# Another order for the opening and step 4 of a fused attention and FFN layer

## The chip, the cores and the metric

The kernel runs on one core of one Trainium2 chip. The metric is the device time of one launch in microseconds, shown as the median of three runs. TensorE (PE) does matrix products, VectorE (DVE) elementwise work and transposes, ScalarE (ACT) activations and copies, GpSimd (POOL) elementwise work, and SyncE (SP) issues all the DMAs of this kernel, one after the other.

## The reference

One post-norm transformer layer on x of shape (8, 1024, 512), all float32:

```python
q, k, v = x @ Wq.T + bq, x @ Wk.T + bk, x @ Wv.T + bv    # 16 heads of 32
q, k = rope(q), rope(k)
qk = einsum('bshd,bstd->bsht', q, k) / sqrt(32)    # heads against heads, at the same position
out = einsum('bsht,bstd->bshd', softmax(qk), v)
out = swapaxes(out, 1, 2).reshape(B, S, E)
x = layernorm(x + out @ Wo.T + bo)
g, u = (x @ gate_w.T) * gate_s, (x @ up_w.T) * up_s    # 512 -> 1408
x = layernorm(x + ((silu(g) * u) @ down_w.T) * down_s)
```

The attention is over the 16 heads of one position, so its matrices are 16 by 16. The projections and the FFN hold most of the arithmetic.

## The kernel before

The 8192 positions are 64 tiles of 128. **Attention** takes two tiles as one unit, 32 units in all. A float32 product is made of three products: each operand is split into a high part (a copy rounded to the matrix type, made by ScalarE) and a low part (operand minus high part), and `project` adds high·high, high·low and low·high over four blocks of the contraction: 12 matmuls of 512 columns for one tile and one weight. A unit needs 96 of them: q, k and v of two tiles (`project_qk`, `project_v`), and the output projection of two tiles (`project_heads`); besides 128 small matmuls of 64 columns for the scores (`score`) and 128 for the weighted values (`weigh_values`).

The work of a unit is spread over five **steps**: step s loads and splits x of unit s, projects and rotates unit s-1, does the softmax and the weighted values of unit s-2, the output projection and the residual of unit s-3, and the norm of unit s-4. Each engine has its own `step` with a fixed order of calls; waits on semaphores (`wait_ge`) tie the engines together, and an engine that waits does nothing that stands behind the wait. `unit_steps` (L78) runs step 4 (`OPENING` is 4) as straight code, then steps 5 to 31 as a hardware loop, then step 32. What steps 0 to 3 would do is written out by hand for each engine: this is the **opening**. In `step` a Python flag `late` changes the order for step 4 alone.

Beside the attention the kernel prepares the **FFN weights**. They arrive in 32 slabs, one in each step. SyncE loads slab m into six operands of `f_all` (`ffn_slabs`); `pieces_of(m)` gives the pieces, 8, 6, 11 and 9 for slabs 0 to 3, and `halved` cuts them further until there are 13 for each slab, so that one semaphore `f_loaded` can be counted in a loop. GpSimd makes four sums (`sums_of_slab`), ScalarE the high parts (`high_of_slab`), GpSimd the low parts (`low_of_slab`, 128x792), ScalarE looks for the largest low part (`top_of_slab`), and SyncE stores high and low parts in four DMAs, which wait for `f_lo_done`, ahead of the loads of the next slab.

Other names that the prediction uses. VectorE: `add_bias` (L1376) takes a projection out of PSUM, `sines` (L1383) is half of the rotation, `turn_k`, `turn_q`, `turn_prob` are transposes, `subtract_top` / `sums_of_prob` / `scale_prob` are the softmax, `low_of_heads` (L1439) makes the low part of the attention's output, `low_of_weight` (L1342) that of a weight (four instructions of 128x512), `add_residual` adds x and takes statistics. ScalarE: `split_x`, `spread_k` (L940), `exponent` (L964), `spread_p` (L980), `high_of_heads`. GpSimd: `rotate` (L1195 and L1201), `low_x` (L1173), `add_output_bias` (L1189), `rstd_of`. `spread_p` makes the operand that `weigh_values` waits for, `spread_k` that of `score`. The number in brackets is the unit, then the tile in it, then the weight (1 is k, 0 is q).

After the attention come eight super steps of the **FFN**, in a Strassen-like scheme of seven products; the change touches none of them.

Of the kernel before, what the change touches and what calls it, by code (L numbers as in the profile page):

```python
# [77 lines left out]
def unit_steps(eng, step, peel, total, tail):  # L78


    for n in range(OPENING, peel):
        step(n)
    with eng.Fori(peel, total) as i:
        step(i)
    for n in range(total, total + tail):
        step(n)
# [18 lines left out]
def post_ln_layer(nc, x_cols, x_rows, rope, w_qkvo, biases, ffn_w, scales, down_s, eye, head_mask, out):  # L105
# [28 lines left out]
    with ExitStack() as ctx:  # L134
# [55 lines left out]
        with ExitStack() as sums:  # L190
# [27 lines left out]
        w_hi_done, w_lo_done = sem("w_hi_done"), sem("w_lo_done")  # L218
# [23 lines left out]
            sem("f_loaded"), sem("f_summed"), sem("f_hi_done"), sem("f_lo_done"))  # L242
        f_hi_stored, f_lo_stored = sem("f_hi_stored"), sem("f_lo_stored")
# [113 lines left out]
        def _(sp):  # L357
# [26 lines left out]
            def first_raw(t):  # L384
                if t == 0:
                    sp.wait_ge(x1_cols_stored, 16 * C * 4)
                    sp.wait_ge(w_lo_done, 4 * KE)
                sp.dma_start(wide[:, t // 4, t % 4], x1_cols[t].rearrange("f e q c -> (f e) (q c)"))\
                  .then_inc(raw_loaded, 16)
# [33 lines left out]
            def ffn_slabs(s):  # L423
                if (m := unit_of(s, 2, UNITS)) is not None:
                    sp.wait_ge(f_lo_done, m + 1)
                    for dn, gu, half, stored in ((dn_hi, gu_hi, f_hi, f_hi_stored), (dn_lo, gu_lo, f_lo, f_lo_stored)):
                        sp.dma_start(dn[:, bass.ds(m * 2 * PART, 2 * PART)],
                                     half[:, 0:2].rearrange("p o c -> p (o c)").bitcast(F32)).then_inc(stored, 16)
                        sp.dma_start(gu[:, :, bass.ds(m * PART, PART)].rearrange("o p c -> p o c"),
                                     half[:, 2:9].bitcast(F32)).then_inc(stored, 16)  # L430
                if (m := unit_of(s, 1, UNITS)) is not None:
                    at_least(sp, f_lo_done, m)
                    for o, at, slab, off, n in halved(pieces_of(m), PIECES):
                        dst = f_all[:, o, at:at + n]
                        sp.dma_start(dst, ffn_w[slab, :, off:off + n]).then_inc(f_loaded, 16)
# [41 lines left out]
            load_rope(3)  # L477
            ffn_slabs(3)
            load_residual(1)
# [137 lines left out]
        def _(pe):  # L617
            def project(out, hi, lo, w, sem_done, first_use, next_av=None):

                for k in range(KE):  # L620
                    if first_use:
                        pe.wait_ge(w_hi_done, KE * W_ORDER.index(w) + k + 1)
                        pe.wait_ge(w_lo_done, KE * W_ORDER.index(w) + k + 1)
                    pe.matmul(out, hi[:, k], w_hi[w][:, k], start=(k == 0), stop=False)  # L624
                    pe.matmul(out, hi[:, k], w_lo[w][:, k], start=False, stop=False)  # L625
                    if k == KE - 1 and next_av is not None:
                        inputs_of_av(next_av)
                    last = pe.matmul(out, lo[:, k], w_hi[w][:, k], start=False, stop=(k == KE - 1))  # L628
                last.then_inc(sem_done, 1)
# [289 lines left out]
        def _(act):  # L919
# [71 lines left out]
            def step(s):  # L991
                late, ending = (isinstance(s, int) and s == n for n in (OPENING, UNITS))
                if not late:
                    slabs(s)
                if (m := unit_of(s, 3, UNITS)) is not None:
                    high_of_heads(m)
                if late:
                    top_of_slab(s - 3)
# [6 lines left out]
                if late:  # L1005
                    high_of_slab(s - 2)
# [21 lines left out]
            spread_p(0)  # L1028
            high_of_slab(0)
            exponent(1)  # L1030
            spread_k(2, 0)
            top_of_slab(0)
            high_of_heads(0)
            split_x(3, 0)
            split_x(3, 1)
            spread_p(1)
            spread_k(2, 1)
            high_of_slab(1)

            unit_steps(act, step, LAGS, UNITS, 1)  # L1040
# [129 lines left out]
        def _(pool):  # L1170
# [15 lines left out]

            def add_output_bias(m, t):
                pool.wait_ge(res_loaded[t], 16 * (m + 1))
                pool.tensor_tensor(res[:, t], res[:, t], bias[:, 3], ALU.add).then_inc(res_added, 1)  # L1189
# [28 lines left out]
            def sums_of_slab(m):  # L1218
                pool.wait_ge(f_loaded, PIECES * 16 * (m + 1))
# [11 lines left out]
            def step(s):  # L1231
                late, ending = (isinstance(s, int) and s == n for n in (OPENING, UNITS))
                if (m := unit_of(s, 4, UNITS)) is not None:
                    rstd_of(m)
                if (m := unit_of(s, 2, UNITS)) is not None and not late:
                    low_of_slab(m)
# [4 lines left out]
                if (m := unit_of(s, 1, UNITS)) is not None:  # L1241
                    rotate(m, 0, 0)
                    if late:
                        sums_of_slab(s - 2)
                    rotate(m, 1, 1)
                    if late:
                        low_of_slab(s - 2)
# [86 lines left out]
        def _(dve):  # L1334
# [9 lines left out]
            def low_x(m, t):  # L1344
                dve.wait_ge(xhi_done, 2 * m + t + 1)
                dve.tensor_tensor(xc_lo[:, t], xc[:, t], xc_hi[:, t].bitcast(F32), ALU.subtract).then_inc(xlo_done, 1)

# [124 lines left out]
            def step(s):  # L1472
                now1, now2, now3, now4 = (unit_of(s, lag, UNITS) for lag in (1, 2, 3, 4))
# [30 lines left out]
                if (m := now1) is not None:  # L1504
# [7 lines left out]
                if (m := now1) is not None:  # L1512
# [52 lines left out]
            sines(2, 1, 0)  # L1565
            turn_prob(1)
            low_of_weight(W_ORDER[3])
# [5 lines left out]
            aggregate(0)  # L1573
            unit_steps(dve, step, LAGS, UNITS, 1)
# [287 lines left out]
```

## Time and profile before

| | us |
|---|---|
| median of 3 runs | 1772.17 (1769.71 to 1772.51) |
| the profiled execution | 1772.28 |
| its span in the trace | 1770.5 |
| PE busy | 1716.3 (97%) |
| DVE busy | 1383.2 (78%) |
| ACT busy | 942.0 (53%) |
| POOL busy | 820.2 (46%) |

The span runs from the first to the last instruction in the trace; the execution's own time is 1.8 us longer. A busy time is the sum over an engine's instructions. The weight loads of TensorE (PEld) overlap its matmuls.

### The profile page before, as it was taken

How to read it: one execution, taken by the hardware profiler on the slowest of the kernel's cores; microseconds unless marked ns; L12 is line 12 of the kernel's file. 1: busy time of each engine (PE TensorE's matmuls, PEld its weight loads, DVE VectorE, ACT ScalarE, POOL GpSimd, SP SyncE). 2: the span in 40 equal slices, each digit the busy share in tenths (PEclk: the TensorE clock that was granted, in tenths of full speed). 3: DMA queues.
4: the chain of work that ended last, by engine and by line, in shares of the span. 5: the costliest groups of instructions: out<-in, count | busy, mean ns of one | idle time of the engine just before them, and what ended most of it. 6: DMA issues, size and time to landing. Idle time of an engine off the chain costs nothing.

```text
span 1770.5 us, 40768 instructions
## 1 busy us (share of the span) xinstructions
PE 1716.3 (97%) x15138; PEld 1404.0 (79%) x15138; DVE 1383.2 (78%) x1978; ACT 942.0 (53%) x1457; POOL 820.2 (46%) x699
## 2 busy tenths in 40 slices
PE   8898999999999999999799999999999999999997
PEld 6677888888888888888578888888888888888886
DVE  7878999999999999999846767677676776767756
ACT  4545545545554554565535455554555545555453
POOL 5778888888888888889300110201102011020112
PEclk9999999999999999999899999999999999999999
DMA  7376776787678877866674452644526445264251
GB/s 209 84 165 156 161 178 166 154 180 176 158 154 202 192 182 170 178 162 136 185 244 134 134 172 80 206 151 133 171 80 204 151 133 172 80 204 151 87 184 63
DMA packets 447191, 278.06 MB, mean 157 GB/s; under 512 B 261408, under 2 KB 385696, under 8 KB 447136
## 3 DMA queue, kind: packets, MB, share of 16 engines
q1 hardware_dynamic: 447136, 277.37, 58.4%
q8 instruction: 30, 0.49, 0.1%
q14 instruction: 25, 0.20, 0.0%
HBM read 183.97 MB, written 93.32 MB: 157 GB/s over the span
## 4 chain that ended last, share of the span: by engine, by line
PE 90%; DVE 4%; issue 3%; DMA 1%; SPq 1%; POOL 1%; ACT 1%; POOLq 0%; DVEq 0%; ACTq 0%
PE ps_x L624 12%; PE ps_x L628 12%; PE ps_x L625 12%; PE ps_s L786 9%; PE ps_s L791 8%; PE ps_x L786 7%; PE ps_x L791 7%; PE ps_x L797 4%; PE ps_x L801 4%; PE ps_s L700 3%; PE ps_a L658 2%; PE ps_a L797 2%; PE ps_a L801 2%; PE ps_s L797 2%; PE ps_s L801 2%
## 5 line engine op out<-in xcount | busy, mean ns | idle before, releaser
L624 PE MATMUL ps_x<-wqkv_hi,xc_hi 128*128 128x512 f32 x768 | 304.9, 397 | 17.2 <-POOL xc_lo L1173 8.1
L1314 POOL TENSOR_TENSOR z<-z,xr 128x512 f32<-128x512 f32 x60 | 77.3, 1315 | 482.9 <-DVE z L1649 482.9
L628 PE MATMUL ps_x<-wqkv_hi,xc_lo 128*128 128x512 f32 x768 | 300.9, 392 | 0.0
L625 PE MATMUL ps_x<-wqkv_lo,xc_hi 128*128 128x512 f32 x768 | 300.6, 391 | 0.0
L786 PE MATMUL ps_s<-x_hi,slot 128*128 128x512 f32 x672 | 265.5, 395 | 8.6 <-DMA slot<-gu_hi 4.7
L791 PE MATMUL ps_s<-x_lo,slot 128*128 128x512 f32 x672 | 262.7, 391 | 0.0
L940 ACT ACTIVATE kX<-kT 32x512 f32<-32x512 f32 x256 | 160.8, 628 | 171.1 <-DVE kT L1399 168.8
L1195 POOL TENSOR_TENSOR qk_cos<-qk_in,rot 128x512 f32<-128x512 f32 x128 | 203.8, 1592 | 73.7 <-DVE qk_in L1376 54.6
L786 PE MATMUL ps_x<-x_hi,slot 128*128 128x512 f32 x560 | 219.6, 392 | 0.9 <-ACT u L1085 0.8
L791 PE MATMUL ps_x<-x_lo,slot 128*128 128x512 f32 x560 | 218.6, 390 | 0.0
L1201 POOL TENSOR_TENSOR qk_cos<-qk_cos,qk_sin 128x512 f32<-128x512 f32 x128 | 202.5, 1582 | 10.6 <-DVE qk_sin L1383 0.7
L624 PEld LDWEIGHTS ps_x<-wqkv_hi,xc_hi 128*128 128x128 f32 x768 | 145.1, 189 | 52.9 <-issue 12.6
L628 PEld LDWEIGHTS ps_x<-wqkv_hi,xc_lo 128*128 128x128 f32 x768 | 145.2, 189 | 30.9
L625 PEld LDWEIGHTS ps_x<-wqkv_lo,xc_hi 128*128 128x128 f32 x768 | 145.4, 189 | 29.4
L786 PEld LDWEIGHTS ps_s<-x_hi,slot 128*128 128x128 f32 x672 | 126.6, 188 | 43.9 <-DMA slot<-gu_hi 5.1
L1580 DVE TENSOR_TENSOR hid<-ps_s,hid 128x512 f32<-128x512 f32 x88 | 60.7, 690 | 128.6 <-ACT hid L1054 128.6
L1308 POOL TENSOR_TENSOR rs<-mv,pw 128x4 f32<-128x4 f32 x16 | 22.5, 1407 | 272.0 <-DVE mv L1669 272.0
L791 PEld LDWEIGHTS ps_s<-x_lo,slot 128*128 128x128 f32 x672 | 126.8, 189 | 25.3
L797 PE MATMUL ps_x<-wd,h 128*128 128x512 f32 x352 | 137.1, 390 | 0.2 <-DVE h L1621 0.2
L801 PE MATMUL ps_x<-wd,h 128*128 128x512 f32 x352 | 137.0, 389 | 0.0
L786 PEld LDWEIGHTS ps_x<-x_hi,slot 128*128 128x128 f32 x560 | 105.5, 188 | 26.5 <-issue 3.2
L791 PEld LDWEIGHTS ps_x<-x_lo,slot 128*128 128x128 f32 x560 | 105.5, 188 | 21.8
(119 smaller groups left out, 3741.4 us busy)
## 6 DMA issues: line engine op xcount, KB each, us to landing
slot<-gu_hi SPq DMA_DIRECT2D x88, 896.0 KB, 5.1
xc<-x_cols SPq DMA_DIRECT2D x32, 512.0 KB, 5.4
v_rows<-v_in SPq DMA_DIRECT2D x32, 512.0 KB, 4.3
v<-v_rows SPq DMA_DIRECT2D x32, 512.0 KB, 5.1
res<-x_rows SPq DMA_DIRECT2D x64, 256.0 KB, 3.6
x_rows<-x_out SPq DMA_DIRECT2D x32, 512.0 KB, 2.8
x_cols<-x_turn SPq DMA_DIRECT2D x128, 128.0 KB, 2.5
wide<-x_cols SPq DMA_DIRECT2D x64, 256.0 KB, 5.2
```

Source lines behind the costliest of these rows:

```text
L624: pe.matmul(out, hi[:, k], w_hi[w][:, k], start=(k == 0), stop=False)
L625: pe.matmul(out, hi[:, k], w_lo[w][:, k], start=False, stop=False)
L628: last = pe.matmul(out, lo[:, k], w_hi[w][:, k], start=False, stop=(k == KE - 1))
L786: pe.matmul(out[:, :], slot[:, WEIGHTS[i], cols], x_hi[:, i, k], start=start, stop=False, skip_group_check=True)
L791: last = pe.matmul(out[:, :], slot[:, WEIGHTS[i], cols], x_lo[:, i, k], start=False, stop=stop, skip_group_check=True)
L797: pe.matmul(out[:, :], h_hi[h][:, rows], wd[:, j], start=first, stop=False, skip_group_check=True)
L801: return pe.matmul(out[:, :], h_lo[h][:, rows], wd[:, j], start=False, stop=last, skip_group_check=True)
L940: last = act.activation(kX[32 * c:32 * c + 32, t, :, c], kT[32 * c:32 * c + 32], ACT.Copy)
L1195: pool.tensor_tensor(qk_cos[:, w].rearrange("p (h d) -> p h d", h=H), qk_in[:, w].rearrange("p (h d) -> p h d", h=H), table_of(m)[:, t, 0] ...
L1201: pool.tensor_tensor(qk_cos[:, w], qk_cos[:, w], qk_sin[:, w], ALU.add).then_inc(rotated[w], 1)
L1314: pool.tensor_tensor(z[:, h, r], z[:, h, r], rows_of_x1(n, h)[:, r], ALU.add).then_inc(z_added[h], 1)
L1580: dve.tensor_tensor(hid2[:, j], bank_y[:, :], hid2[:, j], ALU.add).then_inc(c22_done, 1)
```

## The change

The opening and step 4 are put in another order on ScalarE, GpSimd, VectorE and SyncE; TensorE's order stays, and steps 5 to 32 keep their code, save for the counts of the loads.

- Three of the four low quarters of `wo` are made by GpSimd (`low_of_wo`) between the rotations of units 0 and 1, and the last one by VectorE; they had been four instructions of VectorE in one call. A semaphore of their own, `wo_lo_done`, is waited for by the first `project_heads`, in full from its first block on.
- The loads of slabs 0 to 3 are no longer cut to 13 pieces: 8, 6, 11 and 9 DMAs, with one semaphore for each slab.
- VectorE's opening: `subtract_top(1)`, `sums_of_prob(1)`, `scale_prob(1)`, `turn_prob(1)`, `low_of_heads(0)` stand together, ahead of `add_bias(2, 1, 1)`; `low_of_heads(1)` is done at the end of the opening instead of in step 4.
- Step 4 of VectorE makes the low parts of slab 2 (GpSimd did) and takes `add_bias(3, ·, 2)` in between the transposes.
- ScalarE and GpSimd have step 4 written out by hand. On ScalarE `high_of_heads(1)`, `high_of_slab(1)` and `top_of_slab(1)` stand ahead of `exponent(2)`, and `high_of_slab(2)` ahead of `spread_k(3, 0)`. On GpSimd `sums_of_slab(2)` stands between the two halves of the first rotation of unit 3, and `low_of_slab` is gone from the step.
- SyncE issues `load_residual(1)` ahead of `ffn_slabs(3)`.

```diff
-def unit_steps(eng, step, peel, total, tail):
-    for n in range(OPENING, peel):
+def unit_steps(eng, step, peel, total, tail, first=OPENING):
+    for n in range(first, peel):
...
# SyncE
-                    for o, at, slab, off, n in halved(pieces_of(m), PIECES):
+                    for o, at, slab, off, n in (pieces_of(m) if m < OPENING else halved(pieces_of(m), PIECES)):
                         dst = f_all[:, o, at:at + n]
-                        sp.dma_start(dst, ffn_w[slab, :, off:off + n]).then_inc(f_loaded, 16)
+                        sp.dma_start(dst, ffn_w[slab, :, off:off + n])\
+                          .then_inc(f_first[m] if m < OPENING else f_loaded, 16)
...
             load_rope(3)
+            load_residual(1)
             ffn_slabs(3)
-            load_residual(1)
             store_v(2)
# TensorE, project
-                        pe.wait_ge(w_lo_done, KE * W_ORDER.index(w) + k + 1)
+                        if w < 3:
+                            pe.wait_ge(w_lo_done, KE * W_ORDER.index(w) + k + 1)
+                        else:
+                            pe.wait_ge(wo_lo_done, KE)
# ScalarE, the opening
             spread_p(0)
+            exponent(1)
             high_of_slab(0)
-            exponent(1)
+            high_of_heads(0)
+            top_of_slab(0)
+            spread_p(1)
             spread_k(2, 0)
-            top_of_slab(0)
-            high_of_heads(0)
             split_x(3, 0)
             split_x(3, 1)
-            spread_p(1)
             spread_k(2, 1)
             high_of_slab(1)
-
-            unit_steps(act, step, LAGS, UNITS, 1)
+            high_of_heads(1)
+            top_of_slab(1)
+            exponent(2)
+            normalise_x1(0)
+            high_of_slab(2)
+            spread_k(3, 0)
+            split_x(4, 0)
+            split_x(4, 1)
+            spread_p(2)
+            spread_k(3, 1)
+
+            unit_steps(act, step, LAGS, UNITS, 1, OPENING + 1)
# GpSimd
+            def low_of_wo(k):
+                pool.wait_ge(w_hi_done, KE * 3 + k + 1)
+                pool.tensor_tensor(wo_lo[:, k], w_raw[:, 1, k], wo_hi[:, k].bitcast(F32), ALU.subtract)\
+                    .then_inc(wo_lo_done, 1)
...
             def sums_of_slab(m):
-                pool.wait_ge(f_loaded, PIECES * 16 * (m + 1))
+                if isinstance(m, int) and m < OPENING:
+                    pool.wait_ge(f_first[m], len(pieces_of(m)) * 16)
+                else:
+                    pool.wait_ge(f_loaded, PIECES * 16 * (m - OPENING + 1))
...
-            for t in range(2):
-                rotate(0, t, 1)
-                rotate(0, t, 0)
+            rotate(0, 0, 1)
+            low_of_wo(0)
+            rotate(0, 0, 0)
+            rotate(0, 1, 1)
+            low_of_wo(1)
+            rotate(0, 1, 0)
             rotate(1, 0, 1)
             rotate(1, 0, 0)
+            low_of_wo(2)
             low_x(2, 0)
...
             low_of_slab(0)
+            add_output_bias(0, 0)
+            add_output_bias(0, 1)
             rotate(2, 1, 1)
-            add_output_bias(0, 0)
             rotate(2, 1, 0)
+            sums_of_slab(1)
             low_x(3, 0)
             low_x(3, 1)
-            sums_of_slab(1)
             low_of_slab(1)
-            add_output_bias(0, 1)
-
-            unit_steps(pool, step, LAGS, UNITS, 1)
+            rstd_of(0)
+            rotate(3, 0, 1)
+            add_output_bias(1, 0)
+            sums_of_slab(2)
+            rotate(3, 0, 0)
+            rotate(3, 1, 1)
+            rotate(3, 1, 0)
+            low_x(4, 0)
+            low_x(4, 1)
+            add_output_bias(1, 1)
+            sums_of_slab(3)
+
+            unit_steps(pool, step, LAGS, UNITS, 1, OPENING + 1)
# VectorE, step 4 (late is s == OPENING)
                     sines(m, 1, 1)
+                    if late:
+                        low_of_slab(2)
                     add_bias(m, 1, 0)
                     turn_q(m, 0)
                     sines(m, 1, 0)
-                if (m := now3) is not None:
+                if (m := now3) is not None and not late:
                     low_of_heads(m)
...
                     turn_k(m, 1)
+                if late:
+                    add_bias(OPENING - 1, 0, 2)
+                if (m := now1) is not None:
                     turn_q(m, 1)
+                if late:
+                    add_bias(OPENING - 1, 1, 2)
# VectorE, the opening
             turn_prob(0)
+            subtract_top(1)
             add_bias(2, 0, 0)
             sines(2, 0, 0)
-            subtract_top(1)
+            sums_of_prob(1)
+            scale_prob(1)
+            turn_prob(1)
+            low_of_heads(0)
+            add_bias(2, 1, 1)
             turn_k(2, 0)
-            add_bias(2, 1, 1)
-            sums_of_prob(1)
             sines(2, 1, 1)
             turn_q(2, 0)
-            low_of_heads(0)
+            dve.wait_ge(w_hi_done, KE * 4)
+            dve.tensor_tensor(wo_lo[:, KE - 1], w_raw[:, 1, KE - 1], wo_hi[:, KE - 1].bitcast(F32), ALU.subtract)\
+               .then_inc(wo_lo_done, 1)
             add_bias(2, 1, 0)
-            scale_prob(1)
             sines(2, 1, 0)
-            turn_prob(1)
-            low_of_weight(W_ORDER[3])
             turn_k(2, 1)
             turn_q(2, 1)
             add_bias(2, 0, 2)
             add_bias(2, 1, 2)
             add_residual(0)
             aggregate(0)
+            low_of_heads(1)
             unit_steps(dve, step, LAGS, UNITS, 1)
```

## Rows read from the trace of the kernel before

**Rows 1.** The page: span and instructions.

```profile
span 1770.5 us, 40768 instructions
```

**Rows 2.** Windows: length, busy (instructions) of PE, PEld, DVE, ACT, POOL; PEclk, DMA share, GB/s.

```profile
46.80:85.72 38.92, 31.13 (x610) 24.80 (x608) 34.52 (x42) 21.56 (x35) 33.40 (x28) 0.91 0.37 75
85.72:115.00 29.28, 25.96 (x360) 21.17 (x353) 23.21 (x33) 13.13 (x22) 20.80 (x19) 1.00 0.71 157
115.00:149.60 34.60, 29.18 (x352) 23.42 (x353) 24.71 (x36) 15.74 (x25) 26.31 (x26) 0.90 0.73 179
149.60:175.32 25.72, 25.44 (x352) 21.03 (x353) 23.45 (x33) 13.74 (x22) 19.70 (x18) 1.00 0.58 136
```

**Rows 3.** Timeline of TensorE: start us, us, instruction, [idle before, releaser].

```profile
75.69 2.05 PE L658 MATMUL ps_a<-pX,v 64*32 64x64 f32 x128 [6.60 <-ACT pX L980]
103.74 0.47 PE L624 MATMUL ps_x<-wo_hi,aT_hi 128*128 128x512 f32 x1 [1.38 <-issue]
114.56 0.31 PE L700 MATMUL ps_s<-kX,qT 128*16 128x64 f32 x4 [1.80 <-issue]
136.62 0.65 PE L624 MATMUL ps_x<-wo_hi,aT_hi 128*128 128x512 f32 x1 [3.38 <-issue]
147.53 1.76 PE L700 MATMUL ps_s<-kX,qT 128*16 128x64 f32 x107 [1.74 <-issue]
```

**Rows 4.** Timeline of VectorE in the opening.

```profile
55.73 1.30 DVE L1430 STREAM_TRANSPOSE pT<-prob 128x512 f32<-128x512 f32 x2
58.81 1.21 DVE L1407 TENSOR_REDUCE top<-ps_s 128x64 f32<-128x1024 f32 x1
71.75 1.29 DVE L1430 STREAM_TRANSPOSE pT<-prob 128x512 f32<-128x512 f32 x2
72.97 4.77 DVE L1342 TENSOR_TENSOR wo_lo<-wide,wo_hi 128x512 fp32r<-128x512 f32 x4
```

**Rows 5.** Groups of 40 to 180 us: line, form, count | busy us, mean ns | idle.

```profile
L1195 POOL TENSOR_TENSOR qk_cos<-qk_in,rot 128x512 f32<-128x512 f32 x20 | 32.3, 1617 | 8.7 <-DVE qk_in L1376 8.0 <-DVE kT L1399 0.6
L940 ACT ACTIVATE kX<-kT 32x512 f32<-32x512 f32 x40 | 25.1, 628 | 29.0 <-DVE kT L1399 28.6
L1383 DVE TENSOR_TENSOR qk_sin<-qk_in,rot 128x512 f32<-128x512 f32 x20 | 19.3, 966 | 0.9 <-DVE qk_in L1376 0.4 <-DMA rot<-rope_halves 0.3
L1423 DVE TENSOR_TENSOR prob<-prob,over 128x1024 f32<-128x1024 f32 x5 | 9.6, 1913 | 0.0
L1215 POOL TENSOR_TENSOR f_lo<-f_all,f_hi 128x792 fp32r<-128x792 f32 x6 | 11.6, 1930 | 3.5 <-ACT f_hi L953 3.5
L980 ACT ACTIVATE pX<-pT,own 128x512 f32<-128x512 f32 x20 | 12.8, 712 | 8.0 <-DVE pT L1430 8.0
L1416 DVE TENSOR_REDUCE total<-prob 128x64 f32<-128x1024 f32 x5 | 6.0, 1205 | 1.8 <-ACT prob L964 1.8
L1419 DVE RECIPROCAL over<-total 128x64 f32<-128x64 f32 x5 | 2.8, 553 | 0.2
L1376 DVE TENSOR_TENSOR qk_in<-ps_x,bias 128x512 f32<-128x512 f32 x19 | 12.7, 670 | 3.6 <-PE ps_x L628 2.3 <-issue 1.2
```

**Rows 6.** Timeline of GpSimd.

```profile
45.94 1.30 POOL L1173 TENSOR_TENSOR xc_lo<-xc,xc_hi 128x512 fp32r<-128x512 f32 x1 [2.39 <-ACT xc_hi L923]
119.89 0.38 POOL L1224 TENSOR_TENSOR f_all<-f_all 128x88 f32<-128x88 f32 x1 [6.36 <-DMA f_all<-ffn_w]
```

**Rows 7.** Timeline of SyncE's issues (SPq).

```profile
86.32 7.31 SPq L435 DMA_DIRECT2D f_all<-ffn_w  x13
107.20 0.33 SPq L427 DMA_DIRECT2D dn_hi<-f_hi  x1
109.27 9.11 SPq L435 DMA_DIRECT2D f_all<-ffn_w  x13
```

**Rows 8.** Line 1342 up to 180 us: ns min/median/max, first and last start.

```profile
L1342 DVE TENSOR_TENSOR wqkv_lo<-wide,wqkv_hi x12: 678/692/1785, 5.3 to 23.9; 128x512 fp32r<-128x512 f32 x12
```

**Rows 9.** DMA queues from 112 to 113 us: packets, MB, share of 16 engines.

```profile
q8 instruction: 1, 0.02, 7.6%
```

More of the change, by code:

```diff
@@ L217, in post_ln_layer @@
         w_loaded = [[sem(f"w_loaded{w}_{k}") for k in range(KE)] for w in range(4)]
-        w_hi_done, w_lo_done = sem("w_hi_done"), sem("w_lo_done")
+        w_hi_done, w_lo_done, wo_lo_done = sem("w_hi_done"), sem("w_lo_done"), sem("wo_lo_done")
         const_loaded, halves_made, halves_stored = sem("const_loaded"), sem("halves_made"), sem("halves_stored")
@@ L242, in post_ln_layer @@
             sem("f_loaded"), sem("f_summed"), sem("f_hi_done"), sem("f_lo_done"))
+        f_first = [sem(f"f_first{m}") for m in range(OPENING)]
         f_hi_stored, f_lo_stored = sem("f_hi_stored"), sem("f_lo_stored")
@@ L386, in first_raw @@
                     sp.wait_ge(x1_cols_stored, 16 * C * 4)
-                    sp.wait_ge(w_lo_done, 4 * KE)
+                    sp.wait_ge(wo_lo_done, KE)
                 sp.dma_start(wide[:, t // 4, t % 4], x1_cols[t].rearrange("f e q c -> (f e) (q c)"))\
@@ L991, in step @@
             def step(s):
-                late, ending = (isinstance(s, int) and s == n for n in (OPENING, UNITS))
-                if not late:
-                    slabs(s)
+                ending = isinstance(s, int) and s == UNITS
+                slabs(s)
                 if (m := unit_of(s, 3, UNITS)) is not None:
                     high_of_heads(m)
-                if late:
-                    top_of_slab(s - 3)
                 if (m := unit_of(s, 2, UNITS)) is not None:
@@ L1004, in step @@
                     spread_k(m, 0)
-                if late:
-                    high_of_slab(s - 2)
                 if (m := unit_of(s, 0, UNITS)) is not None:
@@ L1231, in step @@
             def step(s):
-                late, ending = (isinstance(s, int) and s == n for n in (OPENING, UNITS))
+                ending = isinstance(s, int) and s == UNITS
                 if (m := unit_of(s, 4, UNITS)) is not None:
                     rstd_of(m)
-                if (m := unit_of(s, 2, UNITS)) is not None and not late:
+                if (m := unit_of(s, 2, UNITS)) is not None:
                     low_of_slab(m)
@@ L1242, in step @@
                     rotate(m, 0, 0)
-                    if late:
-                        sums_of_slab(s - 2)
                     rotate(m, 1, 1)
-                    if late:
-                        low_of_slab(s - 2)
                     if ending:
@@ L1346, in low_x, with low_of_slab @@
                 dve.tensor_tensor(xc_lo[:, t], xc[:, t], xc_hi[:, t].bitcast(F32), ALU.subtract).then_inc(xlo_done, 1)
+            def low_of_slab(m):
+                dve.wait_ge(f_hi_done, m + 1)
+                dve.wait_ge(f_lo_stored, 2 * 16 * m)
+                dve.wait_ge(lo_seen, m)
+                dve.tensor_tensor(f_lo[:, :, :], f_all[:, 1:10], f_hi[:, :, :].bitcast(F32), ALU.subtract)\
+                   .then_inc(f_lo_done, 1)
             low_of_weight(W_ORDER[0])
@@ L1472, in step @@
             def step(s):
+                late = isinstance(s, int) and s == OPENING
                 now1, now2, now3, now4 = (unit_of(s, lag, UNITS) for lag in (1, 2, 3, 4))
@@ L1500, in step @@
                     turn_k(m, 1)
+                if late:
+                    add_bias(OPENING - 1, 0, 2)
+                if (m := now1) is not None:
                     turn_q(m, 1)
+                if late:
+                    add_bias(OPENING - 1, 1, 2)
                 if (m := now4) is not None:
                     turn_x1(m)
-                if (m := now1) is not None:
+                if (m := now1) is not None and not late:
                     add_bias(m, 0, 2)
@@ L1511, in step @@
                     add_residual(m)
-                if (m := now1) is not None:
+                if (m := now1) is not None and not late:
                     add_bias(m, 1, 2)
```

## The prediction

> **What bounds the kernel now.** I read the engines' busy times first, then windows cut at the step limits of TensorE, then TensorE's timeline for its idle spots, and last the timelines of the engines that these spots wait for. A step of the attention's loop takes 25.72 us and TensorE is busy for 25.44 of them, at full clock [rows 2]: TensorE is the bound, and whatever leaves its chain alone is worth nothing. The three stretches before that are not like this. From 46.80 to 85.72 us TensorE is busy for 31.13 of 38.92 us at a mean clock of 0.91; step 4 takes 29.28 us; step 5, the loop's first pass, takes 34.60 us at 0.90 [rows 2]. So step 4 loses 3.6 us and step 5 loses 8.9 us against a steady step. The losses are single spots [rows 3]: 6.60 us before `weigh_values(1)`, which waits for `spread_p(1)`; 1.38 us before the first matmul of `project_heads(1)`; 1.80 us inside `score(3)`; 3.38 us before `project_heads(2)`; 1.74 us inside `score(4)`. With 0.3 us at the step's end the two spots of step 4 make its 3.6. [...]
>
> **Opening.** The 6.60 us come from VectorE's order. It transposes `prob` of unit 1 only at 71.75 [rows 4], since between `subtract_top(1)` at 58.81 and that transpose it does work for the scores of unit 2. In the new order the chain starts as soon as `turn_prob(0)` is issued, 55.73 + 1.2 = 56.95 [rows 4]. `subtract_top(1)` is two instructions over the same 1024 columns, 2 x 1.2 [rows 4]; `add_bias(2,0,0)` and `sines(2,0,0)`, under which ScalarE's exponent fits, 0.6 + 1.2 (means 0.67 and 0.97 [rows 5], and GpSimd is active); sum and reciprocal 1.2 + 0.5; `scale_prob(1)` 1.9 [rows 5]; `turn_prob(1)` 1.2. That is 56.95 + 9.0 = 66.0. ScalarE has `high_of_heads(0)` and `top_of_slab(0)` behind it by 65.9, and `spread_p(1)` takes four copies of 0.64 to 0.71 [rows 5], so it ends at about 68.8. TensorE ends `project_v(2)` at 75.69 - 6.60 = 69.09 [rows 3]: the stall closes, and with it 1.2 us of half clock that followed it (0.09 of 38.92 us is 3.5, of which most lay in the stall itself).
> What is late next is the last quarter of `wo_lo`. From 66.0 VectorE has `low_of_heads(0)` 1.3, `add_bias(2,1,1)` 0.6, `turn_k(2,0)` 1.0, `sines(2,1,1)` 1.0, `turn_q(2,0)` 0.6, then the quarter, 4.77 / 4 = 1.2 [rows 4]: 71.8. TensorE is through `weigh_values(1)` at 70.5 and waits 1.4. The first `project_heads` then ends at 77.3 (24 matmuls in 5.4 us). Beside it run `add_bias(2,1,0)` (72.5), GpSimd's last rotation of unit 2 (75.2: two instructions, the first 1.6 [rows 5]), `turn_k(2,1)` (74.5), and on ScalarE `spread_k(2,1)`, four of 0.63 [rows 5], to 77.1. So `score(2)` is not held up and ends at 79.3. Step 4 begins 6.4 us earlier than at 85.72.
> GpSimd's three quarters of `wo` cost TensorE little or nothing by place: each goes where GpSimd was idle, as in the 2.39 us before `low_x(2,0)` [rows 6], and takes 1.3 [rows 6]. They do hit VectorE. Its subtraction of a weight takes 692 ns at the median and up to 1785 [rows 8], and the four of `wo` took 4.77 us with GpSimd active [rows 4]. The added ones can hold up at most three such VectorE instructions by 1.1 us each, 3.3 us; at least none, 0. I take 0.5: only the first falls wholly beside two-operand work of VectorE (the last quarters of `wv`), the third falls beside the reductions out of PSUM. Opening: -5.9.
> [...]
>
> **Step 4.** From here on I keep the clock of the trace with step 4 at 79.3. SyncE stores slab 1 once its low parts are done. GpSimd gets to them after `rotate(2,1,0)` (75.2), `sums_of_slab(1)` 1.8, two `low_x` 2.5 and 1.93 for the low parts [rows 5]: 81.5. The four stores take 109.27 - 107.20 = 2.1 us [rows 7]; 11 pieces at 7.31 / 13 = 0.56 each [rows 7] take 6.2 instead of 7.3; data are there 1.5 us after the last issue, as at 119.89 against 109.27 + 9.11 [rows 6, 7]. Slab 2 is there at 91.3. GpSimd waits for it from 88.8 on, with `rotate(3,0,0)`, `rotate(3,1,·)` behind it; ScalarE then makes its high parts (94.0) with `spread_k(3,0)` behind them, and VectorE waits from 91.5 with `low_of_slab(2)`, with all that is left of unit 3 behind it. No row shows that instruction on VectorE: 792 / 512 of 692 ns is 1.1 us, of 1785 ns 2.8 [rows 8]; I take 1.9, what GpSimd needs [rows 5], since a rotation runs beside it. So VectorE is at 95.9 at `add_bias(3,1,0)`, at 99.5 after `turn_prob(2)`, and `spread_p(2)` ends at 102.1. TensorE is through q, k, v of unit 3 at 95.8 (72 matmuls, 16.5 us) and, since `low_of_heads(1)` was done at 81, has no wait before `project_heads(1)` (-1.5, the 1.38 and the switch). It ends that at 101.2 and waits 1.0 for `spread_p(2)`. `spread_k(3,1)` ends at 104.7, just when `score(3)` asks for its second tile. The 1.80 us inside `score(3)` I keep: neither `turn_q` nor `spread_k` ended there, the trace names no releaser, and an instruction fetch of TensorE's kind lies just there [rows 9]; TensorE's code is the same. Step 4: -1.5 + 1.0 = -0.5.
> [...]
>
> **Step 5.** Before, slab 3 landed at 119.89, 4.9 us into the step, and held ScalarE (`high_of_slab(3)` and all behind it) and GpSimd (all rotations of unit 4). Now its loads follow the low parts of slab 2 (95.9) and the stores (2.1 to 4): 9 pieces, 5.0 to 6.3 us by the two rates of rows 7, and 1.5: 105 to 108. GpSimd comes to it at 105.2, after `rotate(3,1,·)`, two `low_x` and a bias. Step 5 begins on TensorE at 79.3 + 28.8 = 108.1. High parts are done by 108 to 110, the low parts by 110 to 112, and the first rotation of unit 4 is asked for at 4 us into the step, 112. So the 3.38 us go, with the half clock behind them (1.7). The other stretch of half clock followed 1.38 + 1.80 us of waits; now 1.0 + 1.80: I take off half of it, 0.85 (bounds 0 and 1.7). The 1.74 stays. Step 5: -3.4 - 1.7 - 0.85 = -5.95. Later steps keep their code and start in the steady state's order: 0.
>
> **Sum.** -5.9 - 0.5 - 5.95 = -12.3. The profiled execution took 1772.28 us (span 1770.5 [rows 1]) and the median of the runs is 1772.17, so nothing is to be shifted: 1760.
>
> **Rivals.**
> 1. *The late slab stays the bound of step 5.* The pieces are fewer, but stores and landing are not shorter, and SyncE has `load_x(4)`, a wait for `v` and the store of x1 ahead of them. For it: slab 3 took 12.7 us from its low parts (107.2) to landing, and 12.7 from 95.9 is 108.6, half a microsecond past step 5's start. Against it: before, that was 4.9 past. If step 5 keeps its 34.60, the time is 1772.3 - 6.4 = 1766.
> 2. *The unnamed waits go too* (no fetch, no half clock, no contention): 1.80 + 1.74 + 0.85 + 0.5 = 4.9 more: 1755. For it: the fetches get more time when TensorE waits elsewhere. Against: TensorE waited 1.4 us shortly before the 1.80 as well.
> 3. *Slower: slab 2 becomes the bound.* VectorE now waits for it in the middle of unit 3. Each us that it lands after 91.3 delays `turn_prob(2)`, `turn_q(3,1)` and TensorE by one. The kernel is slower from 12.3 us on, with a landing after 103.6; at 106 it would take 1775. Against it: even at slab 3's pace (12.7 us from low parts to landing) it lands at 94.2, which gives 1763.
> 4. *The order does nothing*, because VectorE is busy for 34.52 of 38.92 us [rows 2] and contention eats the 3.3 us and more: then only part of the opening's term stays and steps 4 and 5 slip with it; 1768 to 1772.
>
> **Chances.** Forecast 0.58 (1757 to 1764), rival 1 0.17, rival 2 0.17, rival 4 0.05, rival 3 0.03. What a measurement of this kernel can tell from no change is 0.2%, 3.5 us. Faster 0.94, within 0.2% 0.03, slower 0.03. The range is 1752 to 1768: 1752 is rival 2 with a shorter wait for `wo_lo`, 1768 is rival 1 with the full half clock.
>
> **What would show it.** Right: `spread_p(1)` ends by 69.5 and the 6.60 us are gone; a wait of 1 to 2 us before the first `project_heads`; step 4 begins at 79 to 81; slab 2 lands at 91 to 93; idle spots of about 1.8 us inside `score(3)` and `score(4)` still; step 5 takes 28 to 30 us; later steps 25.7. Wrong: a stall of more than 3 us anywhere in step 4 or 5, above all before `project_heads` or `weigh_values`, or steps after 6 that are not 25.7.

## The result and the profile after

The changed kernel takes 1763.07 us, the median of 5 runs (1760.9 to 1764.26), against 1772.33 us: the ratio is 0.9951, 95% interval 0.9940 to 0.9962, so 7 to 11 us less. The profiled execution took 1760.9 us, the fastest of the five, with a span of 1759.1. The traces below therefore have 11.4 us to explain, 2.1 more than the medians differ by.

Windows of the changed kernel, cut where TensorE begins step 4, 5, 6 and 7 (columns as in [rows 2]):

```profile
46.80:84.52 37.72, 33.59 (x613) 26.36 (x611) 31.90 (x44) 21.57 (x35) 33.47 (x29) 0.91 0.38 82
84.52:111.96 27.44, 25.82 (x359) 21.33 (x353) 25.36 (x33) 13.25 (x22) 20.81 (x20) 1.00 0.85 178
111.96:138.89 26.93, 25.71 (x352) 21.17 (x353) 23.66 (x33) 15.87 (x25) 24.41 (x25) 1.00 0.81 198
138.89:164.62 25.73, 25.45 (x352) 21.02 (x353) 23.46 (x33) 13.77 (x22) 20.68 (x19) 1.00 0.68 153
```

Set beside [rows 2]: the opening is only 1.2 us shorter (step 4 begins at 84.52, not 85.72), still with 0.91 of the clock; step 4 is 1.8 us shorter, step 5 is 7.7 us shorter and at full clock; a later step is the same. That is 10.7 us up to step 6; the rest of the span is 0.7 us shorter.

TensorE's timeline, first in the opening:

```profile
70.04 1.44 PE L663 MATMUL ps_a<-pX,v 64*32 64x64 f32 x123 [0.45 <-ACT pX L985]
73.94 0.43 PE L663 MATMUL ps_a<-pX,v 64*32 64x64 f32 x5 [2.47 <-issue]
74.30 0.80 PE L629 MATMUL ps_x<-wo_hi,aT_hi 128*128 128x512 f32 x1
82.59 2.00 PE L705 MATMUL ps_s<-kX,qT 128*16 128x64 f32 x128
...
111.53 0.31 PE L705 MATMUL ps_s<-kX,qT 128*16 128x64 f32 x4 [1.49 <-issue]
136.82 1.76 PE L705 MATMUL ps_s<-kX,qT 128*16 128x64 f32 x107 [0.91 <-issue]
```

The 6.60 us of [rows 3] before `weigh_values(1)` are 0.45. But there is a stall that the kernel before does not have: 2.47 us inside `weigh_values(1)`, after its matmul 123, with no releaser. Then 24 matmuls of the first `project_heads` take 74.30 to 82.59, 8.29 us instead of 5.4, since the granted clock is 0.50 up to 79 us and 0.66 over all of them:

```profile
74.30:82.59 8.29, 8.29 (x27) 6.34 (x25) 3.27 (x5) 3.06 (x5) 6.87 (x8) 0.66 0.14 41
```

The 1.38 and the 3.38 us before `project_heads` of steps 4 and 5 [rows 3] are gone, and the unnamed stalls inside `score(3)` and `score(4)` are still there, at the same matmuls, 1.49 and 0.91 us long.

The other engines. VectorE: the transpose of `prob`, and the two instructions that are new or alone, the last quarter of `wo_lo` and the low parts of slab 2.

```profile
64.78 1.31 DVE L1466 STREAM_TRANSPOSE pT<-prob 128x512 f32<-128x512 f32 x2
70.16 1.13 DVE L1610 TENSOR_TENSOR wo_lo<-wide,wo_hi 128x512 fp32r<-128x512 f32 x1
97.82 2.07 DVE L1381 TENSOR_TENSOR f_lo<-f_all,f_hi 128x792 fp32r<-128x792 f32 x1
```

SyncE: the loads of slabs 2 and 3. GpSimd: where it waits for them.

```profile
86.33 6.21 SPq L436 DMA_DIRECT2D f_all<-ffn_w  x11
101.97 6.25 SPq L436 DMA_DIRECT2D f_all<-ffn_w  x9
```

```profile
93.92 1.05 POOL L1242 TENSOR_TENSOR f_all<-f_all 128x88 f32<-128x88 f32 x1 [0.87 <-DMA f_all<-ffn_w]
111.36 0.37 POOL L1242 TENSOR_TENSOR f_all<-f_all 128x88 f32<-128x88 f32 x1 [2.12 <-DMA f_all<-ffn_w]
```

The transpose of `prob` that stood at 71.75 [rows 4] is at 64.78. Slab 3 is there at 111.36, 0.6 us before step 5 begins, where it had come 4.9 us after [rows 6].

### The profile page after: what moved, and what is told of

It is laid out like the page before. It is cut to its first block, busy times and chain, and to the rows that moved or that the text cites. A ratio compares the mean times of both kernels' runs of the same rounds, so it can differ in the third digit from the quotient of the medians.

```text
span 1759.1 us, 40750 instructions
## 1 busy us (share of the span) xinstructions
PE 1712.2 (97%) x15138; PEld 1400.8 (80%) x15138; DVE 1382.4 (79%) x1976; ACT 942.1 (54%) x1457; POOL 823.4 (47%) x701
## 4 chain that ended last, share of the span: by engine, by line
PE 88%; DVE 4%; issue 3%; DMA 2%; SPq 1%; POOL 1%; ACT 0%; POOLq 0%; DVEq 0%; ACTq 0%
PE ps_x L629 12%; PE ps_x L633 11%; PE ps_x L630 11%; PE ps_s L791 9%; PE ps_s L796 8%; PE ps_x L791 7%; PE ps_x L796 7%; PE ps_x L802 4%; PE ps_x L806 4%; PE ps_s L705 3%; PE ps_a L663 2%; PE ps_a L806 2%; PE ps_a L802 2%; PE ps_s L802 2%; PE ps_s L806 2%
## 5 line engine op out<-in xcount | busy, mean ns | idle before, releaser
L630 PEld LDWEIGHTS ps_x<-wqkv_lo,xc_hi 128*128 128x128 f32 x768 | 144.6, 188 | 28.8
```

## The experiments

All ratios are to the kernel before, timed on the same chip. The experiments were timed on three chips, so times of different experiments are compared by their ratios. The first question was which part brings the time, the second what the 2.47 us are.

**Parts.** `after_step4_old`: step 4 as before on VectorE, ScalarE, GpSimd, the rest as changed.

```diff
# ScalarE
-            high_of_slab(2)
             spread_k(3, 0)
+            high_of_slab(2)
...
# GpSimd
-            sums_of_slab(2)
             rotate(3, 0, 0)
+            sums_of_slab(2)
             rotate(3, 1, 1)
+            low_of_slab(2)
             rotate(3, 1, 0)
+            add_output_bias(1, 1)
             low_x(4, 0)
             low_x(4, 1)
-            add_output_bias(1, 1)
...
# VectorE
-                late = isinstance(s, int) and s == OPENING
+                late = False
...
             aggregate(0)
-            low_of_heads(1)
```

> The changed kernel with step 4 in the old order on VectorE, ScalarE and GpSimd (low parts of slab 2 on GpSimd between the rotations, low_of_heads(1) in step 4, high_of_slab(2) behind spread_k(3,0)); opening, pieces and wo as changed. Theory A (the new order of step 4 is what frees step 5, by getting slab 3 to GpSimd at 111.4 and not 119.9): the low parts of slab 2 come later by some 3 us, slab 3 with them, step 4 gains back a wait of about 1.5 us before project_heads(1), and step 5 takes 29 to 31 us instead of 26.9: 1767 to 1769. Rival (the fewer pieces and the load order free step 5, and the order is worth nothing): 1763.

Measured: 1763.32 us, ratio 0.9956 (0.9943 to 0.9969). The rival's number came, yet TensorE's timeline has waits before `project_heads` in steps 4 and 5; theory A had named the first, at 1.5 us:

```profile
98.51 0.47 PE L629 MATMUL ps_x<-wo_hi,aT_hi 128*128 128x512 f32 x1 [0.65 <-issue]
127.58 0.47 PE L629 MATMUL ps_x<-wo_hi,aT_hi 128*128 128x512 f32 x1 [1.38 <-issue]
```

Its windows up to the starts of steps 4, 5 and 6:

```profile
46.60:81.20 34.60, 30.90 (x612) 24.41 (x610) 31.71 (x43) 20.90 (x33) 33.58 (x29) 1.00 0.40 89
81.20:109.58 28.38, 26.00 (x359) 21.15 (x353) 24.55 (x32) 14.02 (x22) 22.03 (x19) 1.00 0.76 160
109.58:138.61 29.03, 25.98 (x352) 21.14 (x353) 25.31 (x33) 15.87 (x25) 25.95 (x26) 1.00 0.82 202
```

Steps 4 and 5 together take 57.41 us against 54.37, 3.0 us more; the profiled execution made up for it because it had no half clock in the opening and began step 4 3.3 us earlier. So the order of step 4 is worth up to 3 us between these two traces, but the ratios, 0.9956 and 0.9951, do not show it. Another trace says why they need not. `after_nop16` (below) has the order of the changed kernel, the same count of recorded instructions, and full clock in the first `project_heads` too. It has half clock at the start of step 5 instead:

```profile
82.19:110.05 27.86, 25.96 (x359) 21.34 (x353) 25.37 (x33) 14.88 (x24) 22.52 (x24) 1.00 0.86 182
110.05:138.77 28.72, 27.32 (x352) 22.31 (x353) 23.68 (x33) 14.75 (x24) 23.12 (x21) 0.94 0.71 178
```

It begins step 6 at 138.77, `after_step4_old` at 138.61. My theory that step 4's order is what frees step 5 is refuted for the larger part: step 5 falls from 34.6 to 29.0 without it, 5.6 of the 7.7 us. The 29.0 themselves are as the theory had them (29 to 31).

`after_pieces13`: the changed kernel with 13 pieces again; `before_few_pieces`: the kernel before with the fewer pieces alone.

```diff
-                    for ... in (pieces_of(m) if m < OPENING else halved(pieces_of(m), PIECES)):
+                    for ... in halved(pieces_of(m), PIECES):
...
-                    pool.wait_ge(f_first[m], len(pieces_of(m)) * 16)
+                    pool.wait_ge(f_first[m], PIECES * 16)
```

> The changed kernel with slabs 0 to 3 loaded in 13 pieces again. Theory A (what frees step 5 is that slab 3 lands earlier against the step: 0.6 us before its start in the changed kernel, 4.9 after it in the one before; SyncE's issue time is part of that): 2 DMAs more on slab 2 and 4 more on slab 3 at 0.56 to 0.70 each; slab 3 lands some 3 us later, at 2 to 3 us into step 5, which then takes 1 to 2.5 us longer: 1764 to 1766. Rival (the pieces are hidden under SyncE's waits, the order alone does it): 1763.

> The kernel before with 8, 6, 11 and 9 pieces for slabs 0 to 3, and nothing else changed. Theory A: slab 3 lands 2.8 us and more earlier, at 116 instead of 119.9, ScalarE and GpSimd start their part of step 5 that much earlier, and the 3.4 us before project_heads(2) shrink to about 0.5; with the half clock that followed them 4 to 5 us less: 1767 to 1768. The opening is as before. Rival: 1772.

Measured: 1765.31 us, ratio 0.9954 (0.9941 to 0.9967), and 1767.49 us, ratio 0.9972 (0.9961 to 0.9982). On the kernel before, the pieces alone are worth 5 us (3 to 7), and slab 3 is there at 117.7, 2.3 us into step 5 instead of 4.9:

```profile
117.72 0.37 POOL L1229 TENSOR_TENSOR f_all<-f_all 128x88 f32<-128x88 f32 x1 [4.44 <-DMA f_all<-ffn_w]
```

On top of the rest they bring 2.2 us by the medians but 0.5 by the ratios (0.9954 against 0.9951), and the two intervals overlap: that they bring anything there is not shown by the times. In the trace of `after_pieces13` slab 3 is there at 114.88, 1.75 us into step 5.

`opening_and_pieces` and `opening_only`: step 4 old, all four low quarters of `wo` in one VectorE loop where the one stood, and in the second also 13 pieces. They are `after_step4_old` with:

```diff
# GpSimd
-            low_of_wo(0)    # and (1), (2)
# VectorE
-            dve.tensor_tensor(wo_lo[:, KE - 1], w_raw[:, 1, KE - 1], ...)
+            for k in range(KE):
+                dve.tensor_tensor(wo_lo[:, k], w_raw[:, 1, k], ...)
```

> The kernel before with two parts of the change: the new order of the opening (VectorE, ScalarE, GpSimd, SyncE) and the fewer pieces; step 4 in the old order and all four low quarters of wo on VectorE. Theory A (the two account for all of it; step 4's order and wo on GpSimd are worth 1 us or less each): 1761 to 1763. Rival (step 4's order is needed once wo's quarters are back): 1765 and more.

> As the one before, with 13 pieces for slabs 0 to 3 again: of the change only the order of the opening is left. Theory A: pieces alone gave 5 us on the kernel before and 2.2 us on top of the rest; the order alone gives what is left, 1764 to 1767, with slab 3 landing 2 to 4 us after the start of step 5 and a wait before project_heads(2). Rival (without the pieces the late slab takes all that the opening gains): 1770 to 1772.

Measured: 1763.16 us, ratio 0.9955 (0.9942 to 0.9968), and 1764.11 us, ratio 0.9962 (0.9950 to 0.9974). By these ratios the order of the opening alone brings 6.7 us, with the pieces 8.0, and the whole change 8.7; the three intervals overlap, so what the pieces and the rest add to the 6.7 is not told from nothing. These 6.7 and the 5 of the pieces alone add up to more than the whole: both bring slab 3 earlier against step 5. In `opening_only` slab 3 is there at 113.40, 2.2 us into step 5.

`after_wo_dve`: the changed kernel with that second edit only.

> The changed kernel with all four quarters of wo's low parts on VectorE, where the one quarter stands. Theory A (GpSimd's quarters take work off VectorE just before the first project_heads): VectorE needs 2.1 to 3.6 us more there, wo_lo is ready at about 74 to 75 instead of 71.3, TensorE has ended weigh_values(1) at 74 because of the stall inside it: only 0.5 to 1.5 us are lost, and the 0.5 us of contention in the opening come back: 1763 to 1764. Rival (the stall in weigh_values(1) does not hide it): 1766.

Measured: 1760.86 us, ratio 0.9941 (0.9928 to 0.9953). The quarters on GpSimd bring nothing that the times can show; the median is even 2 us lower without them, and lower than the 1763 to 1764 expected, but the intervals overlap. The trace shows the two sides. VectorE's four subtractions of `wv`'s low parts, beside the first GpSimd quarter and without it (the changed kernel, then this one):

```profile
19.26 5.78 DVE L1371 TENSOR_TENSOR wqkv_lo<-wide,wqkv_hi 128x512 fp32r<-128x512 f32 x4
```

```profile
19.35 4.69 DVE L1368 TENSOR_TENSOR wqkv_lo<-wide,wqkv_hi 128x512 fp32r<-128x512 f32 x4
69.12 4.02 DVE L1608 TENSOR_TENSOR wo_lo<-wide,wo_hi 128x512 fp32r<-128x512 f32 x4
```

1.1 us more there, and `weigh_values(0)` starts at 62.40 instead of 61.35. On the other side the last low part is ready at 73.14 instead of 71.29, but the stall in `weigh_values(1)` lasts until 72.90 and its last matmuls until 73.2, so that costs nothing.

**The stall.** Two runs with empty instructions ahead of TensorE's first matmul, 48 and 16, and 48 on the kernel before:

```diff
         def _(pe):
+            for _ in range(48):
+                pe.nop()
```

> The changed kernel with 48 instructions that do nothing ahead of TensorE's first matmul, where TensorE waits for 8 us anyway. Theory A (the 2.46 us inside weigh_values(1), after its 123rd matmul, are a wait for the next block of instruction code; the block before it was entered only some 5 matmuls before weigh_values(1), so the small matmuls ate a whole block in about 2.5 us): 48 instructions move the block's end 24 matmuls earlier, to matmul 99, and then 24 big matmuls more lie in the block, 5 us; the stall shrinks below 0.5 us or goes. If the stretch of half clock over the first project_heads comes from that stall, it goes too: 2.5 + 2.9 = 5.4 us less than the changed kernel, about 1757 to 1758; if the clock does not hang on the stall, 2.5 less, 1760. The stalls inside score(3) and score(4) move by 24 matmuls and stay about as long. Theory B (the stall is a semaphore or data wait of weigh_values(1)): it stays after matmul 123 with 2.5 us, and the time is 1763.

> The changed kernel with 16 empty instructions ahead of TensorE's first matmul; one look. Theory A (block of instruction code): the stalls move 8 matmuls earlier, from 123 to 115 in weigh_values(1), from 124 to 116 in score(3), from 21 to 13 in score(4). The first is shorter by 8 big matmuls, 1.8 us, so 0.5 to 1 us. Theory B (a wait for data or a semaphore): they stay at 123, 124 and 21.

> The kernel before with the same 48 empty instructions. Theory A: there the same block's end lies in weigh_values(1) too, but TensorE waits 6.60 us for spread_p(1) just before, so the fetch is hidden; nothing to gain in the opening: 1771 to 1773, the stalls inside score(3) and score(4) at other matmuls. Theory B: no change either, and the stalls stay at matmul 124 and 21.

Measured: 1762.74 us, ratio 0.9947 (0.9935 to 0.9959); 1762.05 us, a single run; 1772.04 us, ratio 1.0003 (0.9994 to 1.0011). The stalls stayed at matmuls 123, 124 and 21 in the first two, and at 124 and 21 in the third, which has none in `weigh_values(1)`. That is what theory B said, but the edit was no test: the recorded instructions are 40750 as without it (40768 on the kernel before), so it is open whether the empty instructions were in the code at all. So real ones, 24 dummy matmuls:

```diff
                 pe.wait_ge(xhi_done, 2 * m + t + 1)
+                if first:
+                    pe.wait_ge(w_hi_done, 1)
+                    for _ in range(24):
+                        pe.matmul(ps_x[0][0:H, 0:64], xc_hi[:, 0, 0, 0:H].bitcast(F32),
+                                  w_hi[1][:, 0, 0:64].bitcast(F32), start=True, stop=True, ...)
                 pe.wait_ge(xlo_done, 2 * m + t + 1)
```

> The changed kernel with 24 small matmuls (64 columns, into a bank that is overwritten right after) ahead of TensorE's first real one, since empty instructions moved nothing: the stalls stayed at matmuls 123, 124 and 21, and the count of recorded instructions did not change. The dummies take under 1 us where TensorE waits 1.4 us anyway. Theory A (end of a block of instruction code): the stall in weigh_values(1) moves from its matmul 123 to about 99, and as 24 big matmuls (5 us) then lie in that block it shrinks below 0.5 us or goes; those in score(3) and score(4) move to about 100 and out of score(4). The time is 2 us less, 1761, and more where the half clock goes too. Theory B (a wait of weigh_values(1) for data, a semaphore or a bank): the stall stays at 123 with 2 to 2.5 us; 1763.

Measured: 1761.87 us, ratio 0.9938 (0.9925 to 0.9950). The trace decides between the two theories:

```profile
70.73 1.48 PE L663 MATMUL ps_a<-pX,v 64*32 64x64 f32 x128 [0.49 <-ACT pX L990]
72.14 0.50 PE L629 MATMUL ps_x<-wo_hi,aT_hi 128*128 128x512 f32 x1
77.81 2.00 PE L710 MATMUL ps_s<-kX,qT 128*16 128x64 f32 x128
102.73 1.48 PE L663 MATMUL ps_a<-pX,v 64*32 64x64 f32 x128 [0.90 <-ACT pX L990]
107.15 0.98 PE L710 MATMUL ps_s<-kX,qT 128*16 128x64 f32 x52 [1.45 <-issue]
135.21 0.65 PE L710 MATMUL ps_s<-kX,qT 128*16 128x64 f32 x28 [2.01 <-issue]
```

`weigh_values(1)` runs through; the stall of `score(3)` is after matmul 76 instead of 124, that of `score(4)` after 100 instead of 21. The expectation had about 100 for `score(3)`, since it took a dummy for one matmul; in the trace the 24 dummies are 96 recorded instructions, 48 weight loads with their matmuls, and 124 - 48 = 76. In `score(4)` 21 - 48 = -27, and the next spot is 127 further, at 100. In the changed kernel 505 matmuls lie from the stall of `weigh_values(1)` to that of `score(3)` (5, then 24, 128, 72, 24, 128 and 124), four times 126, and 249 from there to that of `score(4)`, two times 124.5. One of the spots between shows in `after_pieces13`, 378 matmuls, three times 126, behind the first:

```profile
108.69 0.30 PE L663 MATMUL ps_a<-pX,v 64*32 64x64 f32 x3 [0.33 <-issue]
```

So the stalls go by the count of instructions, with one possible spot at every 124 to 127 matmuls with their loads; theory B is out.

That instruction code is what TensorE waits for there is an inference: no view names the releaser. Two more facts of the changed kernel's trace speak for it. First, the DMA view has one packet of the queue `q8 instruction` less than 1.5 us ahead of each of the three stalls, in the windows 71.1:71.3, 109:109.2 and 134.5:134.7:

```profile
q8 instruction: 1, 0.02, 37.0%
q8 instruction: 1, 0.02, 36.5%
q8 instruction: 1, 0.02, 28.8%
```

Each stall ends 2.1 to 2.8 us after its packet (at 73.94, 111.53 and 136.82). The second packet is the fourth after the first, as four spots lie between the stalls, and the third is the second after that. Second, that queue has its last packet before 139.0 and none from there to 800 us, and in those passes of the loop the stall is gone: the same matmuls of `score` run through in step 6. This also speaks against stalls that the recording of the trace makes by itself, which would come at the same count of records in every pass.

```profile
162.34 2.00 PE L705 MATMUL ps_s<-kX,qT 128*16 128x64 f32 x128
```

With `project_heads(0)` at full clock, step 4 of `after_dummy24` begins at 79.74. The whole did not gain what the opening did. Its windows of steps 4, 5 and 6, then steps 6 to 31 together and what follows, and the last two of the changed kernel:

```profile
79.74:108.11 28.37, 25.99 (x359) 21.31 (x353) 25.26 (x36) 13.91 (x22) 22.24 (x22) 1.00 0.83 176
108.11:136.04 27.93, 25.73 (x354) 21.16 (x353) 23.70 (x35) 16.00 (x25) 25.41 (x25) 1.00 0.82 198
136.04:161.85 25.81, 25.46 (x352) 21.03 (x353) 23.66 (x33) 13.87 (x22) 19.81 (x18) 1.00 0.68 153
136.04:804.70 668.66, 661.40 (x9152) 546.66 (x9153) 611.37 (x832) 367.40 (x572) 567.92 (x493) 1.00 0.76 171
804.70:1760.50 955.80, 932.14 (x4406) 758.20 (x4402) 654.19 (x994) 501.74 (x773) 144.51 (x110) 0.99 0.46 148
...
138.89:806.80 667.91, 660.98 (x9153) 546.80 (x9153) 610.74 (x832) 367.32 (x571) 568.14 (x494) 1.00 0.76 171
806.80:1759.10 952.30, 929.07 (x4407) 755.88 (x4402) 654.17 (x994) 501.95 (x773) 144.50 (x110) 0.99 0.46 148
```

Step 6 begins 2.85 us earlier than in the changed kernel, and the span after that is 4.3 us longer. The loop has little part in it: its 26 passes take 0.75 us more in all. The other 3.5 us lie behind them, where the dummies change no instruction. There TensorE waits 6.4 us for the load of `slot` instead of 4.3, and the first 53 us have 0.88 of the clock instead of 0.94. The same stretch takes 953.0 us in the kernel before and 950.9 in `wo_dve_dummy8`, so that this loss comes from the dummies is not shown. On the kernel before the same edit was expected to lose:

> The kernel before with the 24 dummy matmuls. Theory A: there the fetch lies under the 6.60 us that TensorE waits for spread_p(1), so nothing is won in the opening; the stalls in score(3) and score(4) move (to 76 and to about 100), and a step of the loop takes 0.09 us more, 2.4 us over 27 steps, as in the changed kernel with them: 1773 to 1775. Rival (the dummies help by something else than the stall): 1770 or less.

Measured: 1774.30 us, ratio 1.0019 (1.0010 to 1.0027), as theory A has it for the opening: the stall before `weigh_values(1)` is still 6.56 us. Its term of 0.09 us for each step of the loop is wrong here too: step 7 takes 25.68 us, and of the 2.2 us that steps 6 to 31 take more 1.6 are in step 6 alone, which has 0.94 of the clock.

`wo_dve_dummy8`: `after_wo_dve` with 8 dummies.

> The changed kernel with wo's low parts on VectorE and 8 dummy matmuls at TensorE's start. By the 24 dummies each one counts as two small matmuls of code (the stall in score(3) moved from its matmul 124 to 76), so 8 of them move the ends of the blocks 16 matmuls earlier: 16 big matmuls, 3.6 us, lie then in the block before weigh_values(1). Theory A (code fetch): the 2.46 us are gone; the stalls of score(3) and score(4) stand at 108 and 5. TensorE is then held by the last low part of wo, which comes at about 73.5 to 74, so 2 us of wait stand before project_heads(0) in place of the stall, and some 0.5 us are won; later steps keep 25.72. 1760 to 1761. Rival (the quarters on VectorE are free, as the median of 1760.9 with all of them there says): the full stall is won, 1758.

Measured: 1760.48 us, ratio 0.9938 (0.9926 to 0.9951), with the stalls at 108 and 5 as foreseen, later steps at 25.74, and the one of `weigh_values(1)` turned into a wait for the last low part of `wo`:

```profile
70.77 1.49 PE L663 MATMUL ps_a<-pX,v 64*32 64x64 f32 x128 [0.42 <-ACT pX L990]
75.05 0.76 PE L629 MATMUL ps_x<-wo_hi,aT_hi 128*128 128x512 f32 x1 [2.80 <-DVE wo_lo L1613]
```

Its first matmul took 0.76 us, against 0.50 in `after_dummy24`, and the granted clock is 0.50 from 75.05 to 77: the half clock came after this wait too. It has the lowest median of all and, with `after_dummy24`, the lowest ratio, by less than the intervals tell apart. Eight dummies with the quarters on GpSimd, where both the stall and this wait would be gone, was not run.

## Why the prediction was right, and where not

The sum was right in kind and near in size: 1760 forecast, 1763.07 the median, 1760.9 the profiled execution; the forecast interval of the likeliest case, 1757 to 1764, holds both. That it came so near is in part luck. The trace has 11.4 us where 12.3 were forecast, but the opening brought 4.7 us less than forecast, and step 4, step 5 and the rest of the span brought 1.3, 1.7 and 0.7 more. Of the prediction's own signs these held: the 6.60 us are gone (0.45 left), no stall in steps 4 and 5 is above 3 us, later steps take 25.7 us, and the idle spots in `score(3)` and `score(4)` are still there, though at 1.49 and 0.91 us. These did not: `spread_p(1)` ends at 70.0 and not by 69.5, there is no wait before the first `project_heads`, step 4 begins at 84.52 and not by 81, slab 2 lands at 93.9 and not by 93, and step 5 takes 26.93 us, not 28 to 30. By its terms, against the trace:

- **Opening, forecast -5.9, measured -1.2.** This is the term that failed. The chain was nearly right: `turn_prob(1)` ends at 66.1, 66.0 forecast, and `spread_p(1)` at 70.0 against 68.8. What I had not seen is in "TensorE is through `weigh_values(1)` at 70.5": it is through at 74.3, for the most part by the stall of 2.47 us, and then `project_heads(0)` runs 2.9 us longer on the half clock. I had kept the 1.80 us of `score(3)` because TensorE's code did not change, and did not ask what other spots of that kind lay under the 6.60 us that I took away: the trace before has one packet of `q8 instruction` in that wait, between 70 and 71 us, and no stall in `weigh_values(1)`. The dummies remove this stall, and step 4 begins at 79.74, where 79.8 was forecast (79.3 and 0.5). That the two agree to 0.1 us is chance: `weigh_values(1)` begins 1.6 us later there than the 69.1 of the forecast, and the forecast wait of 1.4 us for `wo` is not there.
- **The wait for the last quarter of `wo`, forecast 1.4, measured 0.** The quarter is ready at 71.3 (71.8 forecast), and `weigh_values(1)` begins 0.95 us later than forecast, so the quarter is there before `weigh_values(1)` could end, stall or not; in `after_dummy24`, without it, there is no wait. Where the stall is gone and all quarters are on VectorE, 2.80 us of wait come out.
- **Contention, forecast 0.5, measured 1.05** (`weigh_values(0)` 62.40 against 61.35 without the GpSimd quarters). Right in place, half in size: TensorE waited three times for `wv`'s low parts, 0.37, 0.76 and 0.76 us, and once, 0.77 us, without the GpSimd quarters. The third quarter (43.96 to 45.71) fell beside the reduction out of PSUM, as forecast; that took 1.21 us, and it takes 1.19 to 1.23 everywhere in the trace before up to 180 us.
- **Step 4, forecast -0.5, measured -1.8.** Since it begins 4.7 us later than forecast, `spread_p(2)` (105.5) is not late any more and the 1.0 us is not paid; with the dummies 0.90 is, and the step takes 28.37 us against 28.8 forecast. `low_of_slab(2)` on VectorE took 2.07 us (1.9 forecast). Slab 2 was there at 93.9, not 91.3: the stores stand behind `load_residual(1)`, which the change puts ahead of them and which waits for the first `project_heads`, and that ran late on the half clock.
- **Step 5, forecast -5.95, measured -7.7.** In the profiled execution the 3.38 us and both stretches of half clock are gone (I had kept half of one, 0.85), and the 1.74 is 0.91. The two stretches are in the trace before at 116.4 to 119.6 and 136.9 to 140.1, each at a granted clock of 0.50; half of 3.2 us is 1.6 lost in each, where the forecast took 1.7, half of 0.10 of 34.60 [rows 2]. One of these stretches comes and goes: `after_nop16` and `after_nop48` have it, and their step 5 takes 28.72 and 28.89 us, which is -5.9 and -5.7. Slab 3 is there 0.6 us before the step begins, where the forecast had 0.1 to 3 us before it. Rival 1 did not come.
- **Rivals 2, 3, 4.** The unnamed stalls did not go; they shortened by 0.3 and 0.8 us. Nothing was slower.

What is not settled: when the clock falls. Nine kernels with the new opening had the stall in `weigh_values(1)` or a wait in its place, of 2.1 to 2.8 us. In six of their traces the first `project_heads` then runs in part on the half clock, 5 to 12 of its 24 matmuls, in three (`after_nop16`, `after_step4_old`, `after_pieces13`) it does not, after stalls of 2.40, 2.06 and 2.46 us. `after_dummy24`, without a long wait there, had full clock. At the start of step 5, behind the stall of `score(3)`, five of these ten traces have a stretch of half clock (0.94 over the step), and five, with the changed kernel's, have none. That a stall of that kind brings it at times is what the runs show, no more. Every trace is of one execution, so a difference of 2 or 3 us between two traces can be this alone.

## What to carry to other kernels

When you take away a long wait, look at what else lay in its shadow: here a stall without a releaser, known from two other places, came out and, with the slow clock behind it, ate 5 us of the opening. When a queue is the late part, count its instructions first: fewer pieces gave 5.0 us on the kernel before, where the whole change gave 8.7. Parts that each win alone do not add: 6.7 and 5.0 us gave 8.0. And follow a gain to the end of the span: the 2.85 us that the dummies had at step 6 were not there at the end.

## What the runs showed of the chip

TensorE stalls 0.3 to 2.7 us at spots that lie multiples of 124 to 127 matmuls with their loads apart, in straight code and in the loop's first pass, but only where nearly all of the 126 before are matmuls of 64 columns (128 of them in 1.4 to 1.9 us). The spots move with the count of instructions ahead of them (48 pairs more, 48 matmuls earlier). In the changed kernel a packet of the instruction queue comes less than 1.5 us ahead of each of the three stalls, and the stall ends 2.1 to 2.8 us after it. 124 to 127 matmuls with their loads are 249 to 254 recorded instructions. Of the ten packets of that queue from 55 to 139 us in the changed kernel seven came without a stall and three with one.
